# A transformer block pair with experts: key mask and rstd ahead of the bias split on GpSimd, norm ahead of the residual on VectorE, a copy behind four exponentials on ScalarE

## The reference

```python
x = x + tanh(g_xattn[0]) * L0_xattn(layernorm(x), ctx, ctx, mask, w_q, w_k, w_v, w_o)
x = x + tanh(g_ffn[0])   * L0_ffn(layernorm(x), ...)      # 64 experts, 6 a token, and a shared one
x = x + tanh(g_xattn[1]) * L1_xattn(layernorm(x), ctx, ctx, fside, in_proj, out_w, out_b, ...)
x = x + tanh(g_ffn[1])   * L1_ffn(layernorm(x), ...)      # 8 experts, each takes its best 1024 tokens

# L1_xattn, per head
scores = einsum('bhqd,bhkd->bhqk', q, k) * scaling + attention_bias   # a bias per sequence, query and key
attn = softmax(scores); out = einsum('bhqk,bhkd->bhqd', attn, v) * head_scales
return out @ out_w.T + out_b
```

## Time and profile before

| | |
|---|---|
| median of 3 runs | 939.1 us (938.69 to 942.69) |
| the profiled execution | 940.7 us, its span 938.9 us |
| PE busy | 719.0 us (77%) |
| DVE busy | 673.6 us (72%) |
| POOL busy | 611.7 us (65%) |
| ACT busy | 492.1 us (52%) |
| exponentials (L563) | 277.5 us in 1024 instructions |
| key mask (L665) | 63.3 us in 64 instructions, 989 ns each |

### The profile page before, as it was taken

The page is one execution under the profiler, slowest core; times in us unless marked ns, Lnnn a source line. Parts: engine busy times, 40 slices in busy tenths (PEclk is TensorE's granted clock), DMA queues, the critical chain, the costliest instruction groups (busy, mean ns, idle before and its releaser), DMA issues. The chain is left out here.

```text
span 938.9 us, 23770 instructions
## 1 busy us (share of the span) xinstructions
PE 719.0 (77%) x6259; PEld 494.9 (53%) x6259; DVE 673.6 (72%) x2225; ACT 492.1 (52%) x1719; POOL 611.7 (65%) x1109
## 2 busy tenths in 40 slices
PE   3888999999847998358999999999810379879770
PEld 2555556566533666335666666666510157557560
DVE  3787999999966664147888888888769756775334
ACT  2886888878831112037777787777700032432320
POOL 4888666666633676367888888888310376777772
PEclk9999999999967999579999999999955589999895
DMA  6111222222222333133334444333100225665568
GB/s 178 61 66 52 83 83 87 75 75 75 93 66 71 104 106 102 34 114 126 119 118 140 139 142 141 126 125 123 71 12 0 72 52 161 185 167 165 164 182 235
DMA packets 98731, 100.61 MB, mean 107 GB/s; under 512 B 24511, under 2 KB 76077, under 8 KB 98659
## 3 DMA queue, kind: packets, MB, share of 16 engines
q1 hardware_dynamic: 88306, 88.25, 30.2%
q0 software_dynamic: 6656, 9.66, 3.7%
q10 hardware_dynamic: 3696, 1.84, 0.7%
HBM read 60.84 MB, written 44.17 MB: 112 GB/s over the span
## 5 line engine op out<-in xcount | busy, mean ns | idle before, releaser
L563 ACT ACTIVATE P<-bank,mx 128x120 f32<-128x120 f32 x1024 | 277.5, 433 | 4.0 <-DVE mx L865 3.9
L466 PE MATMUL bank<-ident,P 128*120 128x128 f32 x1024 | 167.4, 286 | 41.6 <-ACT P L563 39.3
L466 PEld LDWEIGHTS bank<-ident,P 128*120 128x120 f32 x1024 | 106.1, 138 | 131.2 <-issue 75.2
L865 DVE TENSOR_REDUCE mx<-bank 128x4 f32<-128x480 f32 x256 | 150.5, 650 | 20.8 <-PE bank L455 17.3
L1748 POOL DMA_INDIRECT xg<-token_rows,tokens x64 | 66.7, 1042 | 70.1 <-DVE tokens L1802 51.2
L446 PE MATMUL bank<-bp,identr 128*128 128x480 f32 x256 | 87.3, 426 | 0.0
L1758 POOL DMA_INDIRECT expert_sums<-y,sum_rows x64 | 70.6, 1103 | 23.5 <-issue 18.6
L665 POOL TENSOR_TENSOR Km<-Kf,kmask 128x480 f32<-128x480 f32 x64 | 63.3, 989 | 29.8 <-ACT Kf L547 29.1
L480 PE MATMUL bank<-PT,Vb 120*32 120x128 f32 x2048 | 82.3, 279 | 0.0
L630 POOL TENSOR_TENSOR rstd<-rs,minus_half 128x1 f32<-128x1 f32 x128 | 72.6, 567 | 10.7
L575 ACT ACTIVATE PT<-bank,kept 120x512 f32<-120x512 f32 x64 | 45.2, 706 | 57.8 <-issue 43.0
(11 more groups left out here) (244 smaller groups left out, 1707.7 us busy)
## 6 DMA issues: line engine op xcount, KB each, us to landing
expert_sums<-zeros SPq DMA_DIRECT2D x32, 512.0 KB, 3.4
choice_rows<-zeros SPq DMA_DIRECT2D x32, 384.0 KB, 2.4
yrows<-choice_rows SPq DMA_DIRECT2D x32, 384.0 KB, 3.1
XT<-expert_sums SPq DMA_DIRECT2D x16, 512.0 KB, 5.8
XS<-expert_sums SPq DMA_DIRECT2D x16, 512.0 KB, 5.5
w<-in_w13T SPq DMA_DIRECT2D x8, 704.0 KB, 4.2
token_rows<-payload SPq DMA_DIRECT2D x32, 128.0 KB, 1.7
ctx<-in_ctxT SPq DMA_DIRECT2D x64, 60.0 KB, 2.0
```

Of the source, the lines that this page charges most:

```text
L466: mm = nc.tensor.transpose(TB[r % 2][0:KV, S * j:S * j + S], t.P[:, r, j, :], t.ident[:])
L563: e = nc.scalar.activation(t.P[:, r, j, :], heads(SC[r])[:, j, :], ACT.Exp, bias=t.mx[:, G * r + j:G * r + j + 1], scale=-1.0)
L865: ve.tensor_reduce(t.mx[:, G * r:G * r + G], heads(SC[r]), AX.X, ALU.min).then_inc(ev.mins, 1)
```

## The change

Three edits, all of them in the order in which a `step` lists its work. No instruction is added or taken away, and no operand changes.

- ScalarE, both loops: the four exponentials of group 0 stand ahead of the copy of turned group 3 of the sequence before.
- GpSimd, second loop: the bias split of i+2 is behind the key mask of i+1 and the rstd of i+3, and no longer ahead of both.
- VectorE, second loop: the norm of i+3 and the router's shares stand ahead of the residual and its statistics.

```diff
@@ ScalarE, step
                 here = on(i, 0)
+                if here is not None:
+                    exponentials(here, 0)
                 if on(i, -1) is not None:
                     keep_turned(on(i, -1), 3)
                 if here is not None:
-                    exponentials(here, 0)
                     exponentials(here, 1)
@@ GpSimd, step
                 if L == 1 and on(i, 2) is not None:
                     add_out_bias(on(i, 2))
-                    split_bias(on(i, 2), u)
                 if on(i, 1) is not None:
                     head_keys(on(i, 1), w)
                 if on(i, 3) is not None:
                     rstd(on(i, 3), w, 0, ev.stats1, ev.p1)
+                if L == 1 and on(i, 2) is not None:
+                    split_bias(on(i, 2), u)
@@ VectorE, step (second loop)
                     router_invert(on(i, -4), u, s4)
-                if s1 is not None:
-                    residual(before, w)
-                if s1 is not None:
-                    stats2(before, w, s1)
                 if s0 is not None and not (isinstance(i, int) and i == 0):
                     norm1(on(i, 3), w, s0)
                 if s4 is not None:
                     router1(on(i, -4), u, k, s4)
+                if s1 is not None:
+                    residual(before, w)
+                    stats2(before, w, s1)
```

## The result

The changed kernel takes 965.98 us (median of 4 runs, 965.45 to 966.3), beside 938.89 us (4 runs) of the kernel before on the same chip: a ratio of 1.0272, 95% interval 1.0224 to 1.032. It is slower by 2.7%; the prediction had 961.9 us, within 945 to 970.

What follows compares the result with a forecast made beforehand. No engine is full, so rings of waits between engines set each loop's step. First loop +5.3 us and second loop +17.5 us give +22.8 on 939.1: 961.9 us, range 945 to 970.

Steps and rivals of the forecast that it cites:

- The two rings: Chains of waits setting the step: first loop through TensorE and ScalarE, 7.68 us; second loop through GpSimd and VectorE, 8.94.
- the ring of GpSimd and VectorE: Second loop: output bias, key mask, rstd, norm, shares, residual, second rstd, next output bias; 8.94 us a step, branch included.
- rival 1: Both loops: the rings lengthen but divide and mask do not collide; second loop 8.46 us a step, 949.5 us; chance 0.17.
- (2): Both loops: hardly any effect, since GpSimd has slack; second loop 8.31 us a step, 942 us in all; chance 0.10.
- (3): First loop: faster by 0.27 us a step as ScalarE's idle time absorbs the copy; 930.7 us in all; chance 0.09.
- The collision: Second loop: VectorE's divide waits out GpSimd's key mask, so rstd starts 1.85 us after the output bias; 8.94 against 8.46.
- norm to residual: Second loop, VectorE: the ring's term for norm, shares and whatever follows them, 0.74 us.
- the branch: Second loop: the loop's branch costs GpSimd 0.23 us once in four steps, adding 0.06 us a step to the ring.
- the +0.17: First loop, per step in us: exponentials open with the first minimum, 1.88 after the scores, not turned group 3, 1.71.
- 27 steps of +0.67: Second loop: 27 of 32 steps go from 8.27 to 8.94 us, 18.1 us, less 0.6 for the first step.
- ScalarE's ring in the second loop: Second loop: with the copy behind the exponentials, the ring through ScalarE goes from 8.20 to 8.31 us, +0.11.
- The point that would have shown me wrong: Second loop: divide keeping 0.28 us, residuals 8.3 us apart or less, or norm starting well before project-out is done.

Runs made afterwards that it cites:

- e2: The GpSimd and VectorE edits on the kernel before, ScalarE as before: 1032.82 us, ratio 1.0178, second loop 9.07 us a step.
- e3: The GpSimd edit alone on the kernel before: 1014.18 us, ratio 1.0014, second loop 8.33 us a step.
- e4: The VectorE edit alone on the kernel before: 1050.24 us, ratio 1.0391, second loop 9.95 us a step.
- e8: The kernel before with the GpSimd and VectorE edits and the exponent sums' reciprocals in PSUM: 1018.0 us, ratio 1.0082, second loop 8.69 us a step.
- e1: The ScalarE edit alone on the kernel before: 1027.3 us, ratio 1.0161, second loop 8.76 us a step.
- e10: The kernel before with, in the second loop, VectorE's norm behind the next step's first minimum and the shares ahead of the residual: 1011.97 us, ratio 1.003.
- e5: The changed kernel with the exponent sums' reciprocals in PSUM instead of SBUF: 954.67 us, ratio 1.0179 to the kernel before, second loop 8.70 us a step.

## Why the prediction was right, and where its steps were off

**The two rings.** The first loop's 7.71 us a step and the second's 9.08 stand where the prediction had 7.68 and 8.94. e2 shows that the second loop's loss is the ring of GpSimd and VectorE alone. e3 and e4 tell its halves apart: the residual behind the norm closes the ring (9.95 us by itself), mask and rstd ahead of the split shorten it and put the mask beside the divide (8.33 by itself). The rivals fall: 8.46 us without a collision (rival 1), hardly anything (2), and faster (3), since the minimum does gate the exponentials but later than the turn did.

**The collision.** Of +1.85 us from output bias to rstd, 1.86 came. Its price as a whole, which the prediction put at 8.94 - 8.46 = 0.48, measured 0.38 (e2 against e8), as the ring without it is longer than I had it: 8.69 and not 8.46. One part of that is rstd, which without the collision starts 1.44 to 1.54 us after the output bias and not 1.37.

The rule that the prediction cites from the Trainium skill (SBUF — State Buffer, Who interferes with whom) holds in these traces: two SBUF inputs 0.69 us, one SBUF and one PSUM input 0.27 us, beside the same mask.

**Mis-sized: norm to residual.** I took 0.74 us (norm to the minimum that followed it); a residual follows the shares' copy by 0.21 and not 0.12, and it measured 0.84 (568.00 to 568.84), in the plain steps 0.87. That is 0.13 us too little. Against it stands 0.06 too much from rstd to norm: 0.97 us in a plain step, where the sum had 0.87 + 0.16. With 0.02 us of smaller differences a plain step is 8.97 us and not 8.88.

**Mis-sized: the branch.** In the second loop the changed kernel's plain steps take 8.97 us, and the two behind a branch 0.24 and 0.20 more: 0.11 us a step on average and not 0.06. That is the other 0.05 of the 0.14 us missing in the sum.

In the first loop the terms of the +0.17 were wrong, and only their sum was near. A plain step went from 7.49 to 7.58, only +0.09: scores to minimum was 1.11 (214.17 to 215.28) as read, minimum to exponentials 0.69 and not the 0.77 of the earlier trace rows, where the copy ended last and not the minimum. Each branch took 0.52 us more than a plain step, where before it was 0.10 and hidden by ScalarE's wait for the copy: (0.52 - 0.10) / 4 = +0.10. The prediction named that cost for its upper bound and left it out of its sum.

**Luck: the number of steps.** The second loop's +17.5 us came close to the measured +18.2 by two errors that offset each other. The sum took 27 steps of +0.67. Measured, the 20 intervals from the eighth to the 27th are 0.81 us longer each (16.2 us), the first seven only 0.23 to 0.35 (2.1 us), and the last four together 0.1 shorter; 27 steps of +0.80 would have been 21.6. The same ring is shorter in the steps that are written out at the start: from norm to residual it is 0.31 to 0.67 us there (0.87 later), from GpSimd's second rstd to the next output bias 3.83 (4.08 later), and no branch is in it, so four of these seven went from 8.15 to 8.49. In the first loop it is alike: its 31 intervals are 3.9 us longer together, not 31 x 0.19. The other 0.9 of the +4.8 us came ahead of the first residual, whose start differs by up to 1.9 us between the traces, whatever the edit.

**Wrong, and without effect: ScalarE's ring in the second loop.** The prediction's "from 8.20 to 8.20 + 0.11 = 8.31" carried the first loop's 1.11 us from scores to minimum over to the second loop. There VectorE has residual, statistics, norm and shares ahead of it, and the row stood in the earlier trace rows: minimum at 564.46, 1.50 us after the scores at 562.96. With the 0.69 us from minimum to exponentials the minimum's side is ready at 2.19 us, so putting the copy behind the exponentials was worth 2.19 - 1.77 = 0.42 us and not 0.11. e1 measured 0.41 in a plain step, and 0.48 with the branch. Had only ScalarE been edited, I would have forecast the second loop 12 us short; it was saved by the longer ring beside it.

**The point that would have shown me wrong.** In 28 of the second loop's 32 steps the divide took 0.69 to 0.71 us; it kept some 0.28 to 0.30 only in the first step and the last two. The residuals were 9.06 us apart.

## What to carry over

Where no engine is full, add up the rings, from an instruction to the same one a step later, and let the longest decide: two rings that were each lengthened don't add their losses, and a stall that is no part of the longest ring is free. Moving an instruction ahead of one that another engine waits for puts all that it waits for onto that engine's ring. Read each interval of such a sum in the loop that it is used for, and between instructions of which the second waited for nothing else. Count the steps with the ring as it stands in each of them: the steps written out around a loop can have a shorter one. And an instruction moved to where its own engine has time can still be late for another: the norm behind the first minimum held up the keys through the router's maximum.

## What the runs showed of the hardware

- A divide with two SBUF inputs that starts inside GpSimd's mask takes 0.69 us and ends 0.14 to 0.15 after it; with one input in PSUM 0.27 us (e2, e3 and e8). A small instruction is held too: beside the mask the shares of 128x8 took 0.50 instead of 0.23 us (e10). The mask hardly suffers, 1.04 us for 0.99.
- A hardware loop's branch is no fixed cost: in the first loop its step was 0.10 us longer than the others where ScalarE waited for the copy anyway (before), and 0.52 where it didn't (changed). In the second loop it was 0.29 (8.50 against 8.21) before, and 0.44 over two steps in the changed kernel.
- The three chips on which the stages between and behind the loops take some 70 us more ran the loops in the same time: 7.51 to 7.52 us a step in an unchanged first loop, 9.07 (e2) against 9.08 (changed) and 8.69 (e8) against 8.70 (e5) in the second.
